# Order of a softmax's exponentials, and place of a second norm's statistics, in a one-layer language-model tower

## The reference, cut to what matters

```python
h = W.T[x] + b + pe                                   # embedding
# 1: linear-style attention, 8 heads of 16, with a norm over the causal dots
h = h + attn(layernorm(h))                            # dots, mean and variance by cumulative sums, no softmax
# 2: softmax attention, 2 heads of 64, and a mixture of 8 dense experts
hx = ln_ffn(layernorm(h))                             # the "second norm": a norm of a norm, then gain and bias
q, k, v = hx @ Wq, hx @ Wk, hx @ Wv;  q, k = l2norm(q), l2norm(k)
o = softmax(causal(q k^T)) v ;  y = o @ Wo ;  gate = softmax(y @ gate_W + gate_b)
h = h + sum_e gate_e * (gelu(y @ W1_e + b1_e) @ W2_e + b2_e)
```

## Time and profile before

| | |
|---|---|
| three runs, us | 881.97, 884.92, 888.29 (median 884.92) |
| profiled execution, us | 880.93, its span 879.1 |
| busy, us | PE 793.4, DVE 681.2, ACT 489.0, POOL 334.2 |
| granted TensorE clock, mean | 0.974 |

### The profile page before, as it was taken

The page is one execution under the profiler, slowest core; times in us unless marked ns, Lnnn a source line. Parts: engine busy times, 40 slices in busy tenths (PEclk is TensorE's granted clock), DMA queues, the critical chain, the costliest instruction groups (busy, mean ns, idle before and its releaser), DMA issues.

```text
span 879.1 us, 20865 instructions
## 1 busy us (share of the span) xinstructions
PE 793.4 (90%) x8228; PEld 558.8 (64%) x8228; DVE 681.2 (77%) x1550; ACT 489.0 (56%) x1015; POOL 334.2 (38%) x379
## 2 busy tenths in 40 slices
PE   2799999998767778889899888999999999999997
PEld 1567888777533445555555556777777777777775
DVE  3668888887579755656666437899999999999997
ACT  2435555554345547668678985555555555555553
POOL 6648888666556636546557641000000000000000
PEclk9899999999889969999999999999999999999999
DMA  3201101000000000000000000000000000000000
GB/s 122 54 8 36 35 22 37 25 25 25 0 1 0 2 1 1 2 1 3 2 1 14 2 2 1 1 14 2 13 2 13 2 13 2 13 2 14 1 14 13
DMA packets 9633, 12.02 MB, mean 14 GB/s; under 512 B 1848, under 2 KB 6592, under 8 KB 9536
## 3 DMA queue, kind: packets, MB, share of 16 engines
q1 hardware_dynamic: 8512, 8.59, 3.3%
q0 software_dynamic: 1024, 2.10, 0.9%
HBM read 8.59 MB, written 2.10 MB: 12 GB/s over the span
## 4 chain that ended last, share of the span: by engine, by line
PE 70%; DVE 8%; POOL 8%; issue 7%; ACT 5%; DMA 1%; POOLq 0%; ACTq 0%; DVEq 0%
PE ps L955 68%; POOL room L360 6%; ACT room L541 2%; DVE mx L815 1%; DVE qkn L769 1%; DVE ss L754 1%; ACT room L540 1%; DMA h_all<-emb_rows,idx 1%; POOL ss L327 1%; DVE x L748 1%; PE ps L1035 1%; PE ps L963 0%; DVE ql L777 0%; DVE kl L779 0%; PE ps L983 0%
## 5 line engine op out<-in xcount | busy, mean ns | idle before, releaser
L558 ACT ACTIVATE cst<-ps,col 128x512 f32<-128x512 f32 x256 | 175.7, 688 | 162.0 <-PE ps L955 161.9
L955 PEld LDWEIGHTS ps<-arena,sq 128*128 128x128 f16 x3072 | 192.3, 98 | 61.9 <-DVE sq L939 4.1
L955 PE MATMUL ps<-arena,sq 128*128 128x128 f16 x3072 | 213.0, 219 | 0.8 <-DVE sq L939 0.7
L955 PE MATMUL ps<-y,arena 128*128 128x512 f16 x768 | 207.0, 379 | 1.3 <-DVE och L888 1.3
L939 DVE TENSOR_TENSOR sq<-cst,sq 128x512 f16<-128x512 f32 x256 | 175.6, 686 | 4.4
L360 POOL TENSOR_TENSOR room<-room 128x512 f16<-128x512 f32 (+3 forms) x119 | 118.8, 1013 | 97.9 <-ACT room L541 95.9
L815 DVE TENSOR_REDUCE mx<-ps 128x2 f32<-128x1024 f32 (+2 forms) x76 | 81.7, 1075 | 63.5 <-PE ps L955 63.3
L934 DVE CAST sq<-cst 128x512 f16<-128x512 f32 x256 | 108.6, 424 | 10.8 <-ACT cst L558 3.6
L540 ACT ACTIVATE room<-ps 128x512 f32<-128x512 f32 (+3 forms) x160 | 86.5, 541 | 46.9 <-PE ps L955 46.3
L541 ACT ACTIVATE room<-ps 128x512 f16<-128x512 f32 (+3 forms) x160 | 87.1, 545 | 0.0
L955 PEld LDWEIGHTS ps<-y,arena 128*128 128x128 f16 x768 | 64.6, 98 | 33.1 <-issue 1.8
(11 more groups left out here) (154 smaller groups left out, 1150.3 us busy)
## 6 DMA issues: line engine op xcount, KB each, us to landing
sq<-w_rows SPq DMA_DIRECT2D x16, 256.0 KB
out<-h_all SPq DMA_DIRECT2D x32, 64.0 KB, 1.6
cst<-consts SPq DMA_DIRECT2D x1, 896.0 KB
h_all<-emb_rows,idx POOLq DMA_INDIRECT x32, 4.9
cst<-consts SPq DMA_DIRECT2D x1, 398.0 KB, 3.8
c<-consts SPq DMA_DIRECT2D x1, 256.0 KB
wqkv<-w_qkv SPq DMA_DIRECT2D x1, 192.0 KB
wsm<-w_sm SPq DMA_DIRECT2D x1, 192.0 KB
```

Of the source, the lines that this page charges most:

```text
L558: a.activation(hid[:, f], ps[:, HBANK[f], :], ACT.Gelu_apprx_tanh, bias=col[:, K_B1 + k:K_B1 + k + 1], scale=1.0 / WS).then_inc(S["hid_rea ...
L955: return t_.matmul(o, l, r, start=start, stop=stop, skip_group_check=True)
```

## The change

Three things, in one edit.

1. *Exponentials.* ACT now makes the 32-bit exponentials of both heads first and counts each in a new semaphore `s_used`; then (in steps that have one) `max_row`; then it makes both 16-bit halves by copying `p32` in SBUF instead of a second exponential out of PSUM. PE's scores wait for `s_used` at `2s-1` instead of `p_ready`. `max_row` always uses bank 5, so it waits for the last user of bank 5 and the next output part waits for it; `pair_scores` no longer waits for `max_row`'s copy.
2. *Statistics.* `mv2` and `rr` hold all 16 chunks. `stats2` (with the former `two_norms`) of chunks 0 to 11 moves into the attention steps, between `state_out(c, 1)` and `outputs(c-1)`; `both_norms` follows on POOL at the head of the step after next. Chunks 12 and 13 go in the seam, 14 and 15 in preparing steps 2 and 6.
3. *Seam and preparing steps.* `scaled` moves to the memory of `qkn` and `qk2`; `normed2(0)`, `normed_T(0)`, `project2(0)`, `sum_squares(0)` come earlier, `h1_out(14)` and `outputs(14)`'s followers later, and the rest of attention chunk 15 moves from steps 0 to 3 into steps 1 to 5.

```diff
 # GpSimd
             def step_a(c, nxt, more=2, tail=True):
+                if c >= 3:
+                    both_norms(c - 3)
                 if tail:
                     coefs(c - 1)
...
+            both_norms(NT - 5)
             coefs(NT - 3)
...
-            both_norms(0)
             out_bias(NT - 1)
-            both_norms(1)
+            both_norms(NT - 4)
             coefs(NT - 2)
-            both_norms(2)
             l2_factors(0)
+            both_norms(NT - 3)
             for c in range(NT):
                 if c + 1 < NT:
                     l2_factors(c + 1)
-                if c + 3 < NT:
-                    both_norms(c + 3)
-                if c == 0:
+                if c == 1:
                     coefs(NT - 1)
+                if c == 3:
+                    both_norms(NT - 2)
+                if c == 7:
+                    both_norms(NT - 1)
 # ScalarE, softmax steps
-                        a.activation(p32[:, i % QR, lo:], ps[:, i % 3, lo:], ACT.Exp)
-                        a.activation(phi[:, i % PR, lo:], ps[:, i % 3, lo:], ACT.Exp).then_inc(S["p_ready"], 1)
-                        if s in RAT and i == 2 * s:
-                            max_row(RAT[s])
+                        a.activation(p32[:, i % QR, lo:], ps[:, i % 3, lo:], ACT.Exp).then_inc(S["s_used"], 1)
+                    if s in RAT:
+                        max_row(RAT[s])
+                    for i in (2 * s, 2 * s + 1):
+                        act.wait_ge(S["s_used"], i + 1)
+                        if i >= PR:
+                            act.wait_ge(S["pv_done"], i - PR + 1)
+                        a.copy(phi[:, i % PR, lo:], p32[:, i % QR, lo:]).then_inc(S["p_ready"], 1)
 # VectorE
             def step_a(c, nxt, more=2, first=False):
...
                 state_out(c, 1)
+                if c >= 2:
+                    stats2(c - 2)
                 outputs(c - 1, nxt, first)
...
             masked(NT - 2, 0)
             variances(NT - 3, 1)
             state_out(NT - 2, 0)
-            dve.wait_ge(S["h1_ready"], NT - 3)
-            stats2(0)
-            two_norms(0)
+            normed2(0)
             masked(NT - 2, 1)
             state_out(NT - 2, 1)
+            stats2(NT - 4)
             outputs(NT - 3, 1)
-            stats2(1)
-            two_norms(1)
+            normed2(1)
             h1_out(NT - 3)
             masked(NT - 1, 0)
             variances(NT - 2, 0)
+            sum_squares(0)
+            masked(NT - 1, 1)
+            low_v(0)
+            stats2(NT - 3)
+            outputs(NT - 2, 0)
             dve.wait_ge(S["wlow_ready"], NEARLY)
-            normed2(0)
-            masked(NT - 1, 1)
-            outputs(NT - 2, 0)
-            normed2(1)
-            stats2(2)
-            two_norms(2)
-            h1_out(NT - 2)
-            sum_squares(0)
-            low_v(0)
...
             def step_b(c):
                 unit_qk(c)
+                if c == 0:
+                    h1_out(NT - 2)
+                if c == 5:
+                    h1_out(NT - 1)
...
-                if c == 3:
-                    h1_out(NT - 1)
-                if c + 3 < NT:
-                    if c + 3 >= NT - 2:
-                        dve.wait_ge(S["h1_ready"], c + 4)
-                    stats2(c + 3)
-                    two_norms(c + 3)
                 if c + 1 < NT:
                     low_v(c + 1)
-                if c == 0:
+                if c == 1:
                     variances(NT - 1, 1)
-                if c == 1:
+                if c == 2:
+                    stats2(NT - 2)
+                if c == 3:
                     outputs(NT - 1, 1)
+                if c == 6:
+                    stats2(NT - 1)
 # TensorE
             c, cur = NT - 1, 1
+            normed_T(0)
             for b in range(B):
...
                 if b == 0:
-                    normed_T(0)
-            project2(0)
+                    project2(0)
+            normed_T(1)
...
-            normed_T(1)
             out_T(NT - 2)
+            project2(1)
             out_project(NT - 2)
-            project2(1)
...
                 if s:
-                    pe.wait_ge(S["p_ready"], 2 * s - 1)
+                    pe.wait_ge(S["s_used"], 2 * s - 1)
```

More of the change, by code:

```diff
@@ L130, in tower @@
         st2 = sb("st2", [P, 2, B, 6])
-        mv2 = [sb(f"mv2{i}", [P, B, 2]) for i in range(2)]
-        rr = [sb(f"rr{i}", [P, 2, B]) for i in range(2)]
+        mv2 = sb("mv2", [P, NT, B, 2])
+        rr = sb("rr", [P, NT, 2, B])
         x2_all = sb("x2", [P, 2, B, D])
@@ L176, in tower @@
             vhi_ready vlo_ready qkd_ps hi_ready lo_ready sm_ps sm_used max_link mneg mrow_ps mrow_sb s_ps
-            p_ready plo_pool plo_dve pv_done o_link o_used oT_ps oT_sb y_ps yhi_ready ylo_ready
+            s_used p_ready plo_pool plo_dve pv_done o_link o_used oT_ps oT_sb y_ps yhi_ready ylo_ready
             lg_ps lg_link lg_ready eg_ready gate_ready gT_ps gT_sb b2_ps h2_ready hid_ps hid_ready hhi_ready
@@ L279, in weights_low, with both_norms @@
                                 piece[:, :, 0, :], ALU.subtract).then_inc(S["wlow_ready"], 1)
+            def both_norms(c):
+                pool.wait_ge(S["stats2"], c + 1)
+                g.tensor_tensor(rr[:, c, 1], rr[:, c, 0], mhalf[:, 0:B], ALU.pow).then_inc(S["rr_ready"], 1)
             front(0, 0)
@@ L500, in step_b @@
                 high_qk(c)
-                if c == 2:
+                if c == 4:
                     ao_out(NT - 1)
@@ L510, in max_row @@
                 act.wait_ge(S["mrow_ps"], it + 1)
-                a.copy(qm[:, it % 2], ps[:, row_bank(it), :]).then_inc(S["mrow_sb"], 1)
+                a.copy(qm[:, it % 2], ps[:, 5, :]).then_inc(S["mrow_sb"], 1)
             def out_part(m, j):
@@ L704, in masked, with stats2 @@
                                 upper.unsqueeze(1).to_broadcast([P, HA, P]), ALU.mult).then_inc(S["dt_sb"], 1)
+            def stats2(c):
+                par = c % 2
+                dve.wait_ge(S["h1_ready"], c + 1)
+                for b in range(B):
+                    last = v.bn_stats(st2[:, par, b], h_all[:, 2 * c + b, :])
+                last.then_inc(S["st2_link"], 1)
+                dve.wait_ge(S["st2_link"], c + 1)
+                for b in range(B):
+                    last = v.bn_aggr(mv2[:, c, b], st2[:, par, b])
+                last.then_inc(S["agg2"], 1)
+                dve.wait_ge(S["agg2"], c + 1)
+                v.tensor_scalar(rr[:, c, 0], mv2[:, c, :, 1], 1.0 + LN_EPS, LN_EPS * LN_EPS, ALU.mult, ALU.add
+                                ).then_inc(S["stats2"], 1)
             def step_a(c, nxt, more=2, first=False):
@@ L726, in _ @@
                     step_a(c + u, 1 - u)
[L728 to L742, removed]
             def normed2(c):
@@ L1081, in normed_T @@
                 pe.wait_ge(S["x2_ready"], c + 1)
+                if c == 0:
+                    pe.wait_ge(S["qkT_sb"], NT)
+                if c == 1:
+                    pe.wait_ge(S["sgc_ready"], 2 * NT - 2)
                 if c == 2:
@@ L1095, in project2 @@
                 pe.wait_ge(S["hxT_sb"], c + 1)
+                if c == 0:
+                    pe.wait_ge(S["qkv_sb"], 2 * NT)
                 if c == 1:
@@ L1143, in step_b @@
                     project2(c + 2)
-                if c == 1:
-                    pe.wait_ge(S["hxT_sb"], 4)
+                if c == 3:
+                    pe.wait_ge(S["hxT_sb"], 6)
                     out_T(NT - 1)
-                if c == 2:
-                    pe.wait_ge(S["hxT_sb"], 5)
+                if c == 4:
+                    pe.wait_ge(S["hxT_sb"], 7)
                     out_project(NT - 1)
@@ L1195, in max_row @@
             def max_row(it):
-                nonlocal guard
+                nonlocal bank5
                 pe.wait_ge(S["mneg"], it + 1)
-                if it and guard:
-                    pe.wait_ge(*guard)
+                if it:
+                    pe.wait_ge(*bank5)
                 for r in range(4):
-                    last = mm(ps[:, row_bank(it), r * P:(r + 1) * P], mpad[:, r].rearrange("p h e -> p (h e)"), minus16)
+                    last = mm(ps[:, 5, r * P:(r + 1) * P], mpad[:, r].rearrange("p h e -> p (h e)"), minus16)
                 last.then_inc(S["mrow_ps"], 1)
                 if it:
-                    guard = S["mrow_sb"], it + 1
+                    bank5 = S["mrow_sb"], it + 1
             def scores(s):
@@ L1315, in _ @@
             pe.wait_ge(S["wlow_ready"], NPIECE)
-            pe.wait_ge(S["p_ready"], 2 * NSTEP)
+            pe.wait_ge(S["s_used"], 2 * NSTEP)
             pe.wait_ge(S["sm_used"], NMAX)
```

24 lines of the change are left out of this document (8 added, 16 removed).

## The result

The changed kernel takes 878.55 us (median of 6 runs, 876.78 to 881.29) against 885.32 (881.97 to 888.29) of the kernel before. The medians lie 6.8 us apart; the recorded ratio of the runs is 0.9938, 95% interval 0.9917 to 0.9959, so 3.6 to 7.3 us faster, 5.5 in the middle. Forecast were 870 and -12.5 us. The time lies in the range of 862 to 882, but the gain is about half of the forecast. The profiled execution took 878.74 us, its span 876.9.

What follows compares the result with a forecast made beforehand. PE's matmuls (68% of the span) were taken as the bound, with gains only from PE's waits and clock. 0.5 - 4.6 - 1.0 - 7.4 = -12.5 us from 880.93 gives 868.4, carried by +2.0 to 870; range 862 to 882.

Steps and rivals of the forecast that it cites:

- Attention steps, +0.5: Attention steps: the moved statistics mostly fit into idle time of DVE and POOL, costing 0.5 us.
- The collision with POOL at 884: Attention steps, rival: moved scalar operation stands behind POOL's instruction each step, 14 us in all, total 884; chance 0.08.
- Seam, -4.6: Seam: PE's waits for `normed2(0)` (2.10 us) and `unit_qk(0)` (2.53 us) vanish, gaining 4.6 us.
- The ceiling of 4.65: Seam: PE's whole idle time in that stage's window, 31.00 - 26.35, taken as the most that could be gained.
- Preparing steps, -1.0: Preparing steps: with 0.87 us off DVE the chain bounds eight steps, 0.12 us gained in each, 1.0 in all.
- The first six, for which 0 was taken: First six preparing steps: moved rest of attention chunk 15 and low clock taken to net 0, between -4 and +4.
- Maxima's row, -4.2 + 1.5: Softmax steps: PE's 4.2 us of waits behind the row's copy vanish; a new bank 5 wait costs 1.5.
- The new wait for L518: Softmax steps 7, 15, 23: `max_row` waits for ACT's copy out of bank 5, 0.5 us each, +1.5.
- Exponentials, -2.0 - 3.2 + 0.5: Softmax: copies replace second exponentials; single earlier steps gain 2.0, 18 late steps 3.2, the stage's end costs 0.5 us.
- slower rival: Softmax steps: later first-head half delays POOL's subtraction and PE each time, 27 us, total 897; chance 0.08.

Runs made afterwards that it cites:

- e8: Changed kernel with the second exponential back in place of the copy, only the maxima's row kept in bank 5: 871.35 us, ratio 0.9864.
- e3: Changed kernel with ACT's order exponential, copy, exponential, copy, so both heads' high halves come as far apart as before: 878.64 us, ratio 0.9940.
- e9: Changed kernel with heads swapped between VectorE and GpSimd and the gates ahead of the subtraction in VectorE's queue: 869.87 us, ratio 0.9848.
- e7: Changed kernel with the heads swapped between VectorE and GpSimd for making the low halves: 869.87 us, ratio 0.9850.
- e5: Changed kernel with an output part's gates ahead of the step's subtraction in VectorE's queue: 874.17 us, ratio 0.9887.
- e2: Kernel before with the softmax part alone (copy for second exponential, maxima's row in bank 5, scores waiting for `s_used`): 887.13 us, ratio 1.0031.
- e6: Changed kernel with eight useless matmuls in front of PE's wait for the last gates at step 71: 876.64 us, ratio 0.9922.

## Why the prediction was wrong

- **Attention steps, +0.5: right.** From step 4 to step 13 the two timelines keep their distance of 3.07 us to 0.01. The collision with POOL at 884 did not come; the 170 ns at most of `rr` show it.
- **Seam, -4.6: right,** -5.24. It came at the place named. The ceiling of 4.65 was read too low: its window ended at 232.00, inside the second wait, and up to the first `unit_T` PE idled 5.92.
- **Preparing steps, -1.0: right for its eight steps.** Steps 6 to 14 took 31.14 us instead of 32.31 (-1.17). The first six, for which 0 was taken, gave the rest: 29.39 instead of 30.33 behind the first `unit_T`, at a granted clock of 0.83 against 0.78.
- **Maxima's row, -4.2 + 1.5: the first half right, the second wrong.** Its wait gave 0.46 + 0.69 + 0.67 + 0.70 + 1.03 = 3.55 us. The new wait for L518, charged with 1.5, is not among the waits of the changed kernel or of e8; only e3 shows it, once, with 0.64 us at step 15.
- **Exponentials, -2.0 - 3.2 + 0.5: the step that failed.** The working of ACT's step was right: 2.01 to 2.03 us where nothing else is late, against 2.04 forecast, and 2.81 us gained in steps 62 to 78 of e9 against 3.2. The single steps (13, 19, 21, 29, 41, 53, 61) gave 2.6 against 2.0, the end cost 0.79 against 0.5. What failed is that VectorE's subtraction was charged with nothing. The prediction followed the later 16-bit half to POOL's L360 only, as its slower rival, and found 0.8 us of waits there (1.9 after). But POOL's start is not what the order moves most: VectorE's subtraction began 0.94 us behind POOL's before and 0.48 after, so it now runs into it, and behind it in VectorE's queue stand the row maxima, the output parts and the gates. That cost 4.1 us in steps 22, 30, 32, 42 and 66, where PE waits for VectorE, 2.6 at step 71, and 4.3 of clock behind it in this execution. Another 0.8 in step 55 is a wait for POOL's subtraction (0.7), the rival that the prediction had named, at a small price.
- **The lock of the port pair was used at the wrong place.** The prediction weighed the page "SBUF — State Buffer" of the Trainium skill for the statistics, where the scalar operation met no collision, and not for the two subtractions of one step. There e3 and e7 show that VectorE's length hangs on when it starts against POOL's, and e5 what stands behind it. With the order of the heads turned, e7 gains 13.2 us. That it comes so near to the forecast's 12.5 is luck in part, since the stages ahead of the softmax gave 2.1 us more than forecast in the profiles and the clock's part changes from execution to execution.

Open: steps 0 to 11 of the softmax take 38.88 to 44.29 us in the ten other profiles, at a granted clock of 0.68 to 0.93 in the first seven, with no order that follows the edits. The differences of the profiles there (-1.27) are not put down to the change. Open too is why the clock, behind the same waits, falls for a longer or a shorter time (steps 72 to 75 after and in e2) or not at all (the experts' start after and in e6).

## What to carry to other kernels

When two instructions are put closer together on one engine, look at who consumes both, and whether the consumers lie on VectorE and GpSimd: let the shorter one, VectorE's, start first. Behind a drawn-out instruction count what its queue still holds for TensorE, and cost a wait of TensorE twice, once as a wait and once as what its clock takes afterwards; the second price is the less certain (4.3 us in one profile, 1.6 in another). A change in several parts is worth running part by part: here one part carried more than the whole gain, and one reordering ate half of it.

## What was not expected of the hardware

- An operation of 0.19 us on VectorE took 1.16 when it started 0.04 us behind one of GpSimd's; a subtraction of 0.69 took 1.23 when it started 0.48 behind. In the other order, GpSimd's starting 0.57 us behind, the two took 0.69 and 1.16.
- One idle time of PE of 2.50 us was followed by about 10 us at the lower clock, 4.3 us in price; in e2 one of 2.49 by about 5 us, 1.6 in price. Eight useless matmuls in the gap kept the clock up (e6). Behind waits of 0.35, 0.92 and 1.33 us the clock was up in one execution and down in another (2.75 against 4.34 us for the same twelve matmuls).
- ACT's step of two exponentials and two copies took 2.01 us in pairs of a kind and 2.29 in alternation (e3). The operations are the same, but in e3 each copy waits for the exponential right ahead of it: it starts 0.62 us behind it, where two exponentials of a pair start 0.49 apart.
